# Rows of a scatter buffer 144 floats long instead of 130, in a conv, attention and mixture-of-experts kernel

## The reference

```
x = conv_block(x)        # group norm, qkv, 4-head softmax attention over 1024 pixels, projection, + x
t = tokens(x)
t = t + linear_attention(layernorm(t))                 # 8 heads
t = t + experts(layernorm(t))

experts: probs = softmax(xt @ Wr + br); top 2 of 8 experts for each token
         xn    = layernorm(xt)
         y_e   = gelu((xn * ln_g[e] + ln_b[e]) @ W1[e] + b1[e]) @ W2[e] + b2[e]      # 128 -> 512 -> 128
         out   = the weighted sum of the two chosen y_e
```

## Time and profile before

| what | value |
|---|---|
| median of three timed runs | 363.25 us (363.18 to 363.31) |
| the profiled execution: span from its first to its last instruction | 384.2 us |
| the profiled execution's own time | no figure apart from the span is given |
| busy: PE, PEld, DVE, ACT, POOL | 87%, 55%, 53%, 53%, 29% of the span |
| granted TensorE clock, mean | 0.929 |
| DMA, software queue q0 | 3744 packets, 10.31 MB |
| DMA, hardware queue q1 | 16808 packets, 18.04 MB |
| the two writes of empty rows (L478) | 1495.0 KB each |
| the 46 loads of tiles (L378) | 65.0 KB each |

### The profile page before, as it was taken

How to read it: one execution, slowest core, us unless ns; L and a number is a source line. 1 busy time by engine, 2 the same in 40 slices (tenths; PEclk the granted TensorE clock), 3 DMA queues, 4 the chain that set the end, 5 groups by cost and what they waited for, 6 DMA issues and landing times.

```text
span 384.2 us, 6582 instructions
## 1 busy us (share of the span) xinstructions
PE 334.2 (87%) x2004; PEld 211.5 (55%) x2004; DVE 202.1 (53%) x616; ACT 204.4 (53%) x324; POOL 110.8 (29%) x140
## 2 busy tenths in 40 slices
PE   7879799899999989999998496967551999999996
PEld 3533343333333335445432354867551999999996
DVE  2584444563756553565576248666402455777620
ACT  1460765666576554655585023665212677777732
POOL 2082291000000001000307630061774344444430
PEclk9985989999999999999999879996665899999999
DMA  6078768660000025000001102010211222222415
GB/s 186 2 149 194 170 146 333 154 243 34 0 2 3 3 72 149 0 2 1 2 0 43 55 8 62 16 28 23 62 62 34 64 72 70 71 66 79 143 37 210
DMA packets 21772, 29.28 MB, mean 76 GB/s; under 512 B 4055, under 2 KB 15628, under 8 KB 21484
## 3 DMA queue, kind: packets, MB, share of 16 engines
q1 hardware_dynamic: 16808, 18.04, 17.7%
q0 software_dynamic: 3744, 10.31, 8.4%
q10 hardware_dynamic: 1188, 0.53, 0.6%
HBM read 11.62 MB, written 9.25 MB: 54 GB/s over the span
## 4 chain that ended last, share of the span: by engine, by line
PE 70%; DVE 13%; issue 6%; another core or an unknown queue 4%; ACT 3%; DMA 1%; POOL 1%; DVEq 0%; SPq 0%; ACTq 0%; POOLq 0%
PE ps L864 15%; PE ps L1081 10%; PE ps L1068 9%; PE ps L845 6%; PE ps L826 6%; DVE above L1189 4%; PE ps L706 2%; PE ps L806 2%; PE ps L922 2%; PE ps L746 2%; PE ps L899 2%; PE ps L778 1%; PE ps L891 1%; DMA Qs<-mrow 1%
## 5 line engine op out<-in xcount | busy, mean ns | idle before, releaser
L558 ACT ACTIVATE probs<-ps 128x1024 f32<-128x1024 f32 x64 | 65.3, 1021 | 37.0 <-PE ps L845 36.9
L1081 PE MATMUL ps<-w,GT 128*128 x368 | 55.0, 297 | 18.8 <-ACT GT L684 15.0
L864 PE MATMUL ps<-probs,vT 128*32 128x512 f32 x256 | 68.2, 608 | 1.1 <-ACT probs L558 1.1
L864 PE MATMUL ps<-probs,ones 128*32 128x512 f32 x256 | 68.2, 609 | 0.0
L1081 PEld LDWEIGHTS ps<-w,GT 128*128 128x128 f32 x368 | 49.3, 208 | 22.0 <-issue 21.7
L1189 DVE CUSTOM_DVE_ANT_0 above<-ps,above 128x512 f32<-128x512 f32 x56 | 38.7, 691 | 40.8 <-PE ps L826 39.0
L496 POOL DMA_INDIRECT token_out<-Y,yidx x46 | 44.2, 961 | 48.2 <-DVE Y L1480 46.6
L433 POOL TENSOR_TENSOR rstd<-ve,minus_half 128x1 f32<-128x1 f32 (+2 forms) x6 | 10.3, 1724 | 160.6 <-DVE ve L1231 88.6
L1068 PE MATMUL ps<-XTT,w1s 128*128 128x128 f32 x368 | 53.1, 291 | 3.2 <-issue 3.2
L684 ACT ACTIVATE GT<-H 128x512 f32<-128x512 f32 x46 | 28.9, 629 | 46.5 <-DVE H L1469 27.4
L1068 PEld LDWEIGHTS ps<-XTT,w1s 128*128 128x128 f32 x368 | 49.2, 208 | 4.3 <-issue 4.3
(11 more groups left out here) (196 smaller groups left out, 427.5 us busy)
## 6 DMA issues: line engine op xcount, KB each, us to landing
expert_in<-zeros POOLq DMA_DIRECT2D x2, 1495.0 KB, 7.6
XR<-expert_in SPq DMA_DIRECT2D x46, 65.0 KB
Qs<-q_hi SPq DMA_DIRECT2D x16, 128.0 KB, 3.1
w<-in_L_ffn_W SPq DMA_DIRECT2D x1, 2048.0 KB, 8.4
w<-in_L_ffn_W SPq DMA_DIRECT2D x8, 256.0 KB, 4.1
YG<-token_out SPq DMA_DIRECT2D x8, 256.0 KB, 4.1
Ks<-k_hi SPq DMA_DIRECT2D x14, 128.0 KB, 2.6
X<-in_x SPq DMA_DIRECT2D x2, 512.0 KB, 4.6
```

The lines of the kernel that those rows point to most:

```text
L558: nc.scalar.activation(probs[:, s % 3, :], bank(2 + 2 * (s % 2), 2), ACT.Exp).then_inc(exp_done, 1)
L864: last = nc.tensor.matmul(bank(6 + o % 2)[i * HD:(i + 1) * HD, :], w, probs[:, s % 3, hd * HALF:(hd + 1) * HALF], start=kt == 0, stop=kt = ...
L1081: last = nc.tensor.matmul(bank(4 + p)[:, 0:D], GT[:, p, c, :], w2[:, e, c, :], start=c == 0, stop=c == HC - 1)
```

## The change

The length of a row, `RW`, goes from 130 to 144 floats, so from 520 to 576 bytes. Everything that is shaped by it grows along: `zeros`, `X2`, `XR`, and the DRAM tensor. Floats 130 to 143 of a row are read by nobody, but they are copied with the row. So that they hold a number, a memset of floats 128 to 143 of every row of `X2` is put on GpSimd, ahead of the iotas.

```diff
-    RW = D + 2
+    RW = D + 16
...
             pool.wait_ge(xs_zeroed, 16 * B)
 
+            link(nc.gpsimd.memset(X2[:, :, :, D:RW], 0.0))
             for b in range(B):
                 link(nc.gpsimd.iota(X2[:, b, :, D], [[2, J]], base=2 * b * L, channel_multiplier=2 * J,
```

## The result

| | median | lowest to highest | runs |
|---|---|---|---|
| before, on the same chip | 363.31 us | 361.85 to 364.68 | 19 |
| after | 365.22 us | 362.65 to 366.34 | 20 |

A twentieth run of before, at 412.49 us, lies far above all others and is left out. The ratio is 1.0045, with a 95% interval from 1.0029 to 1.0062. That is 1.6 us slower (1.05 to 2.25); the medians lie 1.9 us apart. The forecast of 364.3 us has the right sign and is 0.9 us short of the median. The runs of after fall into two groups with nothing between them: 8 from 362.65 to 364.11 us, and 12 from 364.99 to 366.34.

A forecast was written before the change was run, and what follows sets the result against it. PE, busy 87% of the span, was taken to bound the kernel, with a wait for maxima behind the empty rows' writes. Memset 0.28 + writes 0.80 = 1.08 us on 363.25 gives 364.3 us; eight-in-ten range 363.3 to 365.8.

The forecast's parts named there:

- The place and the mechanism: First layer, first pair's second half: the maxima land only when GpSimd's empty-row writes are through; PE idles 1.12 us.
- The terms of the sum: Memset +0.28 us and writes +0.80 us at PE's wait for the maxima: 1.08 us, between 0.21 and 1.34.
- The memset: Memset of the empty rows on GpSimd, directly ahead of their writes: 322 more elements on a partition, +0.28 us.
- the writes: The two DMA writes of empty rows grow from 3.06 to 3.39 MB, 7.43 to 8.23 us of each engine: +0.80 us.
- The wait: PE's idle time at the maxima, ahead of the scores, grows from 1.12 to 2.20 us.
- the whole amount is carried: The 1.08 us added at PE's wait for the maxima reaches the kernel's end in full.
- Rival one: After PE's longer idle time the clock falls to half, +1.25 us on top: 365.6 us; chance 27%.
- The fall's price: Half clock behind PE's wait costs +1.25 us, from exponentials 4.19 us apart against 2.94 in the same loop.
- Rival two: PE's wait for the maxima isn't lengthened: 363.25 us, up to 363.9; chance 22%.
- The rule on which it leaned: DMA engines go round between queue rows packet by packet, so the maxima wait one empty-row packet at most each turn.
- the 3.8 us: From 62.8 to 66.6 us the DMA engines move no packet of the hardware queue, on which the maxima wait.
- Rival three: Aligned 576-byte rows speed up the empty-row writes, so PE's idle time shrinks: 362.1 us at most gain; chance 8%.

The follow-up runs named there:

- wider buffers: The kernel before with rows of 130 floats, but X2 and XR laid out with a pitch of 144: 363.26 us, 1.0007.
- after, longer: A second profiled execution of the kernel after, no edit: 366.39 us, span 364.6 us.
- 26 rows: The kernel before with 26 empty rows of 130 floats on each partition in place of 23: 365.25 us, 1.006.
- 31 rows: The kernel before with 31 empty rows of 130 floats on each partition in place of 23: 369.09 us, 1.0169.
- second profile: The kernel before, unchanged, profiled and timed again: 363.10 us, 1.0003; PE did not wait for the maxima.
- experiments 2 to 5: Empty rows' writes moved later (on after 0.9995, on before 0.9984) or earlier (on after 1.000, on before 0.999), ratios to the kernel before.
- experiment 2: The kernel after with the writes of empty rows held back until the maxima mrow_in[3] have landed: 362.88 us, 0.9995.

## Why the prediction was right in kind, and where its size was off

**The place and the mechanism held.** The maxima stand behind the empty rows, and PE's wait for them is where the row's length shows. It goes with the writes moved either way, it comes back with larger writes of short rows, and it does not come with wider buffers.

**The terms of the sum held.** The memset grew by 0.27 us (forecast 0.28), the writes by 0.76 us of each engine (forecast 0.80). The wait grew from 1.12 to 2.19 (forecast 2.20) in the execution that started up as the profiled one of before did. The distance from the issue of the writes to PE's start is a check that doesn't hang on the start-up:

| kernel | MB written | writes issued | scores start | between |
|---|---|---|---|---|
| before | 3.06 | 58.12 | 68.33 | 10.21 |
| wider buffers | 3.06 | 56.85 | 67.05 | 10.20 |
| after | 3.39 | 57.47 | 68.44 | 10.97 |
| after, longer | 3.39 | 58.43 | 69.45 | 11.02 |
| 26 rows | 3.46 | 57.36 | 68.47 | 11.11 |
| 31 rows | 4.13 | 58.02 | 70.70 | 12.68 |

From 3.06 to 4.13 MB that is 2.3 us for each MB, so 0.76 us for the 0.33 MB of this change, whatever the rows' length.

**The step that failed: "the whole amount is carried", from one profile.** I took the 1.12 us of idle time as a property of the kernel. It is one of an execution. By the profiles PE waits for (writes issued + the distance above) - (maxima issued + 4.5), where that is above zero: 4.5 us is what PE still has to do after the maxima's issue (62.73 to 67.21 in before, where the idle time begins). With the writes 4.6 us ahead of the maxima before waits 1.1 us; with them 6.0 ahead, as in its second profile, it doesn't. Started up as after was in its own profile, before wouldn't wait either by this rule (writes issued near 57.2, scores free to start at 67.4, PE there at 67.53), and after waits 0.9 us. So the first part of the added time is covered there, and less than the sum is carried.

**Rival one was no alternative, but the other part of a mixture.** I gave the falling clock 27%, as something that happens or doesn't. It happens in some executions. Where both starts are as in the first profile of before, the change costs 1.1 + 2.3 = 3.4 us by the first scatter (202.59 to 206.04). Where they are as in after's own, it costs 0.8 by the rule above. The measured 1.6 lies between. That the forecast of +1.1 lies so near it is in part luck: it left out a cover that makes the cost smaller and a fall that makes it larger. If only these two kinds existed, some 3 in 10 runs would be of the dear one, and 5 of the 20 runs lie above 365.9 us, near the longer execution. No profile shows one of the seven from 364.99 to 365.60; a short fall as in the kernel with 31 rows would fit. The timed runs speak for it: the mean granted clock is 0.953 in all twelve of the upper group, and 0.957 or 0.958 in six of the eight of the lower one; 3.4 us at half clock take some 1.7 / 364 = 0.005 off the mean. With the writes moved away (experiments 2 to 5), 4 of the 48 runs have 0.953 and none has less. But a mean does not say where the clock fell (the second profile of before has 0.953 and no fall here), so this is argued and not shown. The fall's price of 1.25 us was right for 3.4 us of half clock and half of what the longer execution paid.

**Rival two,** the unchanged wait, is out, and its condition is not: there are executions where before has the maxima on time, but after doesn't. The rule on which it leaned (the Trainium skill, "DMA: Bandwidth & Descriptors", section Queues, rings and completion order) I had read too narrowly. It says that an engine drains a whole packet of typically 9 to 17 descriptors from a ring before it goes on to the next. What the profile counts as packets of q0 here are 288 pieces, 18 for each engine: 256 of 13.2 KB in after, one partition's 23 rows each, and for each write 16 small ones at its end. If these are the rule's descriptors, the two writes are one or two turns of each engine, and the trace agrees with it. But I had also read more into the 3.8 us than they say. With nothing in the way, in experiment 2, the first packet of the maxima comes 1.2 us after their issue (64.17 after 62.97), so in before it could not have come ahead of about 63.9, and the first write's small pieces are through by 63.7. The first 1.1 of the 3.8 us would have held no packet of theirs anyway, and what they stood behind is the rest of the second write. Whether they would have been let in between the two writes, no run here shows.

**Rival three,** faster by aligned rows, is out: the writes' rate did not change (2.3 us for each MB at either row length).

## What to carry to other kernels

A small transfer on a critical path shouldn't be issued while a bulk write from another queue is under way: here it waited until the write under way was through, so the bulk's size, by floats nobody reads too, became time. Move the bulk to where no engine waits for a transfer; here either side did. And before a wait of one microsecond is priced from a profile, take a second profile: where two engines race, its length is a matter of the execution, and an added microsecond of idle time can bring the half clock with it.

## What the runs showed of the hardware that was not expected

- *The start-up varies.* In the profiles of these kernels, in which PE does the same up to there, the maxima were issued between 61.47 and 63.98 us, and the memset of the empty rows began between 53.67 and 54.98.
- *Idle time and clock.* The 2.19 us of idle time in a dense stretch were followed by half clock for 6.8 us (2.4 us lost), and 3.19 us by half clock for 3.4 us (1.2 us lost). After 0.91 to 1.12 us at the same place the clock stayed at 1.00.
- *Scatters on the chain.* Without the long pieces of the earlier trace rows, GpSimd's scatters stand on the chain ahead of the normalisation's `rstd`. The last steps in the chain of after:

```profile
219.22 0.96 POOL expert_in L492
...
220.20 1.70 POOL rstd L433
...
221.93 1.21 DVE F L1240 x4
```

Sixteen issues at 0.96 us and 0.30 us between two would make 20 us. Fourteen of them, 17.6 us, stand ahead of `rstd` (202.65 to 220.20), DVE waits 3.66 us for it, and PE 2.18 us for DVE. The row's length doesn't touch this. An order with `rstd` ahead of the scatters might win up to about 2 us, an estimate from PE's wait, and was not tried.
